# Keeping attention's results transposed, and dividing by the softmax sums on GpSimd

## The chip, the cores and the metric

One program runs on one core of a Trainium2 chip. The metric is the device time of one execution in microseconds (us); the kernel before takes 2816.75 us (median of 3 runs). The core has TensorE (PE; its weight loads are shown as PEld), VectorE (DVE), ScalarE (ACT), GpSimd (POOL) and SyncE (SP, which here only issues DMAs); 16 DMA engines serve them all.

## The reference

A gated cross-attention layer and a two-layer mixture of experts, in float32, on x of shape (8, 512, 256) and a context of shape (8, 1601, 128). What matters here is the attention; it has 16 heads of 16 columns:

```
q, k, v   = heads(x @ Wq + bq), heads(x @ Wk + bk), heads(x @ Wv + bv)
y         = softmax(causal(q k^T / 4)) v                    # SELF
qc, kc, vc = heads(x @ Wcq + bcq), heads(ctx @ Wck + bck), heads(ctx @ Wcv + bcv)
y         = y + softmax(qc kc^T / 4) vc                     # CROSS
x         = x + tanh(g_xattn) * (y @ Wp + bp)
x         = x + tanh(g_ffn) * experts(layernorm(x))         # router, 6 experts top 2, 2 shared, twice
```

Each softmax is computed as exponentials, a product with v, and a division of the result by the sum of the exponentials.

## The kernel before

It has four stages with a barrier between them: `stage_project` (projections to DRAM), `stage_attend`, `stage_mix` (the product with Wp, the layernorm, the first router, and the preparation of expert weights) and `stage_experts`.

`stage_attend` works on 32 items; an item is one batch and a group of 4 heads. The keys of an item are 17 tiles: 13 of context (CROSS, s = 0 to 12) and 4 of x itself (SELF, s = 13 to 16). One list `events`, written by `item_events`, sets the order of TensorE, and VectorE and ScalarE walk the same list. For each tile s, in two halves:

- ST (L847) computes scores transposed, keys on rows; ScalarE's `exp` (L804) takes the exponential into one of three buffers P.
- AV (L862) multiplies with V on TensorE into the PSUM bank OP. V has 16 columns of values and 16 columns of ones for each head, so OP has, on rows 32h to 32h+15, the results of head h transposed, and on rows 32h+16 to 32h+31 its sum, 16 times the same row. OP is [128, 512]: rows by query tokens.
- MAX (L835 and L823, L828) computes scores of the *next* item once more, tokens on rows, into one of the two PSUM buffers R, only for VectorE to take their maxima (L755, L752). 32 such tiles are for CROSS, spread over s = 0 to 12, and 8 for SELF. SHIFT transposes the maxima (L892), which VectorE writes as two rows (L769, L771) that SyncE's DMAs put under the queries (L664).
- OUT, twice an item, for CROSS at (s, half) = (14, 0) and for SELF at (1, 0) of the next item: ScalarE has copied OP to SBUF (`O`, L812); TensorE transposes it back in four pieces (L896) into a buffer R, which it shares with MAX and SHIFT in the order of the list; VectorE takes the reciprocals of the sums, now a column of each head (L776, `den`), and multiplies (L781, `yk`). GpSimd adds the two kinds (L743, `ysum`), and SyncE stores the item (L669) in `y_rows`, tokens on rows.

GpSimd otherwise copies the values into V (L724) and sets the future part of SELF's diagonal tiles to zero (L738), which AV waits for. SyncE's queue has the loads of the item after the next, the shift rows and the stores in one order. At the end a barrier waits for all stores.

In `stage_mix` a block is one batch. Event A loads y (L1125, tokens on rows), transposes it on TensorE in 8 pieces into the PSUM tile `tp` (L1357); ScalarE writes the high part yH (L1310), VectorE the rest yL (L1220). F and FB combine expert weights (L1366, L1377), O multiplies y by Wp (L95 to L97) and VectorE adds and normalises, T transposes the normalised x in two halves through one PSUM tile `xt` (L1403; high part L1323, rest L1258), and G computes the router's logits (L946). The second half of T waits until VectorE has read the first from `xt`.

Of the kernel before, what the change touches and what calls it, by code (L numbers as in the profile page):

```python
# [13 lines left out]
ACT = mybir.ActivationFunctionType  # L14
# [3 lines left out]
P = 128  # L18
# [3 lines left out]
KC = C // P  # L22
# [503 lines left out]
def stage_attend(nc, a, QS, KS, VS, YS, XS, XR, idf, idm, mqm, first):  # L526
# [6 lines left out]
    with ExitStack() as ctx:  # L533
# [9 lines left out]
        O = [r_.sb(f"O{k}", [P, T]) for k in range(2)]  # L543
        den = r_.sb("den", [P, 2, QT, G])
        yk = [r_.sb(f"y{k}", [P, QT, G, D]) for k in range(2)]
        ysum = [r_.sb(f"ysum{u}", [P, QT, GC]) for u in range(2)]
# [9 lines left out]
        (s_v, s_st, s_ex, s_msk, s_av, s_fill, s_drain, s_oe, s_ya, s_pm, s_sr, s_rc) = (  # L556
            r_.sem(n) for n in ("v", "st", "ex", "msk", "av", "fill", "drain", "oe", "ya", "pm", "sr", "rc"))
# [31 lines left out]
        def item_events(n):  # L589
# [3 lines left out]
            for s in range(NKT):  # L593
                for half in range(2):
# [30 lines left out]
        events += [("AV", NI - 1, LAST, halves(LAST)[-1]), ("OUT", NI - 1, SELF)]  # L625
# [4 lines left out]
        slot = {e: k for k, e in enumerate(x for x in events if x[0] in ("MAX", "SHIFT", "OUT"))}  # L630

        with nc.Block() as block:

            @block.sync
            def _(sp):
# [31 lines left out]
                def store(n):  # L667
                    sp.wait_ge(s_ya, n + 1)
                    sp.dma_start(YS[n // NG, :, :, n % NG * GC:(n % NG + 1) * GC], ysum[n % 2][:, :, :]).then_inc(s_yst[n % 2], 16)  # L669
# [14 lines left out]
                for n in range(NI):  # L684
# [20 lines left out]
            def _(pool):  # L705
# [24 lines left out]
                ones(2)  # L730
                for n in range(NI):
                    if n + 1 < NI:
                        values(n + 1)
                    for s in range(CTXT, NKT):
# [5 lines left out]
                    pool.wait_ge(s_drain, slot["OUT", n, SELF] + 1)  # L740
                    if n >= 2:
                        pool.wait_ge(s_yst[n % 2], 16 * (n // 2))
                    pool.tensor_tensor(ysum[n % 2][:, :, :].rearrange("p t c -> p (t c)"),  # L743
                                       yk[0][:, :, :, :].rearrange("p t h d -> p (t h d)"),
                                       yk[1][:, :, :, :].rearrange("p t h d -> p (t h d)"), ALU.add).then_inc(s_ya, 1)

            @block.vector
            def _(dve):
# [25 lines left out]
                def output(n, kind, buf):  # L774
                    t = buf[:, 0, :].rearrange("p (q h e) -> p q h e", q=QT, h=G)
                    dve.reciprocal(den[:, kind], t[:, :, :, D]).then_inc(s_rc, 1)  # L776
                    dve.wait_ge(s_rc, 2 * n + (2 if kind == SELF else 1))
                    if n >= 1:
                        dve.wait_ge(s_ya, n)
                    dk = bcast(den[:, kind].rearrange("p q (h o) -> p (q h) o", o=1), D, 2)  # L780
                    dve.tensor_tensor(yk[kind][:, :, :, :].rearrange("p q h d -> p (q h) d"),  # L781
                                      t[:, :, :, 0:D].rearrange("p q h d -> p (q h) d"), dk, ALU.mult
                                      ).then_inc(s_drain, 1)

                for e in events:
                    if e not in slot:
                        continue
                    k, n = slot[e], e[1]
                    dve.wait_ge(s_fill, k + 1)
                    if e[0] == "MAX":  # L790
                        reduce_tile(n, e[2], k, R[k % 2])
                    elif e[0] == "SHIFT":
                        shift_parts(n, e[2], k, R[k % 2])
                    else:
                        output(n, e[2], R[k % 2])

            @block.scalar
            def _(act):
# [8 lines left out]
                for e in events:  # L807
                    if e[0] == "ST":
                        exp(e[1], e[2], e[3])
                    elif e[0] == "AV" and e[2] in (CTXT - 1, LAST) and e[3] == halves(e[2])[-1]:  # L810
                        act.wait_ge(s_av, av_done[e[1:3]])
                        act.activation(O[kind_of(e[2])][:, :], OP[:, :], ACT.Copy).then_inc(s_oe, 1)  # L812

            @block.tensor
            def _(pe):
# [52 lines left out]
                for e in events:  # L868
# [4 lines left out]
                    if e[0] == "AV":  # L873
                        values(n, e[2], e[3])
                        continue
                    k = slot[e]
# [10 lines left out]
                    elif e[0] == "SHIFT":  # L887
# [5 lines left out]
                    else:  # L893
# [162 lines left out]
def stage_mix(nc, a, YS, X1S, XS, XR, w, BR, SEL, R, tg, idf):  # L1056
# [5 lines left out]
    with ExitStack() as ctx:  # L1062
# [3 lines left out]
        y = [r_.sb(f"y{u}", [P, QT, C]) for u in range(2)]  # L1066
# [11 lines left out]
        tp = r_.ps("tp", [P, KC, T])  # L1078
        op = r_.ps("op", [P, QT, C])
        comb, bias, xt = r_.ps("comb", [P, KC, IW]), r_.ps("bias", [P, KC]), r_.ps("xt", [P, T])  # L1080
# [4 lines left out]
        s_xb, s_T, s_yH, s_yL, s_op, s_x1, s_st, s_ag, s_var, s_rs, s_nm, s_xf = (  # L1085
# [950 lines left out]
```

## Time and profile before

| | us |
|---|---|
| runs (3) | 2814.58, 2816.75, 2819.35; median 2816.75 |
| the profiled execution | 2810.69 |
| its span, first to last instruction | 2808.6 |
| PE busy, in the span | 2489.5 (89%) |
| DVE busy | 1931.8 (69%) |
| ACT busy | 1576.7 (56%) |
| POOL busy | 478.8 (17%) |

The span is what the trace covers; the time of an execution has about 2 us around it. Busy time is a mean over stages with different limits, so the rows below take the stages and then one item of attention by themselves. A line such as L896 is a line of the kernel before.

### The profile page before, as it was taken

To read this page: it belongs to the slowest core of one execution; us is meant where nothing else is said; L and a number is where in the kernel's file an instruction comes from. 1 tells how busy PE (TensorE), PEld (TensorE's weight loads), DVE (VectorE), ACT (ScalarE), POOL (GpSimd) and SP (SyncE) were. 2 spreads that over 40 slices of the span, in tenths; PEclk is the share of its full clock that TensorE was granted. 3 is DMA by queue.
4 is the path that set the end of the run, shared out by engine and by line. 5 is a ranking of instruction groups with operands and counts; after the bars stand their busy time and mean duration, and the time that the engine had idled before them with its cause. 6 is when DMAs were issued, how large, how long until landed. Compare 5 with 4: busy or idle time off the path is not lost. (4 is left out here: it accounts for less than half of the span.)

```text
span 2808.6 us, 55075 instructions
## 1 busy us (share of the span) xinstructions
PE 2489.5 (89%) x20166; PEld 1507.6 (54%) x20166; DVE 1931.8 (69%) x3187; ACT 1576.7 (56%) x3345; POOL 478.8 (17%) x541
## 2 busy tenths in 40 slices
PE   7886999999999999999999998767599968969896
PEld 6773444444444444444444444666487857857675
DVE  8776888888888888888888882544234534634546
ACT  4440777777777777777777776322144423423432
POOL 2002000101010100000010102222303141340413
PEclk9996999999999999999999998768799989989998
DMA  7999757565665647475655623311234312321433
GB/s 267 400 359 237 96 81 104 77 90 75 91 83 85 88 71 104 70 105 67 92 82 85 81 40 90 129 63 57 75 92 120 92 68 61 110 90 35 147 98 98
DMA packets 164962, 305.70 MB, mean 109 GB/s; under 512 B 45607, under 2 KB 112334, under 8 KB 156366
## 3 DMA queue, kind: packets, MB, share of 16 engines
q1 hardware_dynamic: 151358, 265.56, 45.4%
q0 software_dynamic: 12288, 33.57, 3.8%
q10 hardware_dynamic: 1072, 3.23, 0.5%
q8 instruction: 163, 2.67, 0.4%
q14 instruction: 81, 0.66, 0.1%
HBM read 165.13 MB, written 127.68 MB: 104 GB/s over the span
## 5 line engine op out<-in xcount | busy, mean ns | idle before, releaser
L804 ACT ACTIVATE at_P<-at_ST 128x512 f32<-128x512 f32 (+4 forms) x2176 | 1095.9, 559 | 371.8 <-PE at_ST L847 349.5
L755 DVE TENSOR_REDUCE f_part<-at_R 128x2 f32<-128x804 f32 x1024 | 976.0, 994 | 121.1 <-PE at_R L835 117.1
L862 PE MATMUL at_OP<-at_P,at_V 128*32 128x256 f32 x8192 | 641.4, 385 | 16.0 <-ACT at_O L812 12.9
L847 PE MATMUL at_ST<-at_Q,at_K 64*128 64x512 f32 (+4 forms) x1428 | 343.9, 455 | 3.5 <-ACT at_P L804 3.5
L862 PEld LDWEIGHTS at_OP<-at_P,at_V 128*32 128x32 f32 x8192 | 163.1, 108 | 264.0 <-ACT at_P L804 186.7
L835 PE MATMUL at_R<-at_K,at_Q 64*128 64x402 f32 x1344 | 271.0, 392 | 5.1 <-DVE f_part L755 5.1
L738 POOL TENSOR_SCALAR_AFFINE_SELECT at_P<-at_P 128x512 f32<-128x512 f32 x128 | 81.6, 637 | 1088.8 <-ACT at_P L804 1088.8
L847 PEld LDWEIGHTS at_ST<-at_Q,at_K 64*128 64x128 f32 (+1 forms) x1428 | 141.7, 180 | 218.5 <-ACT at_P L804 203.6
L752 DVE TENSOR_REDUCE f_mx<-at_R 128x2 f32<-128x256 f32 (+3 forms) x256 | 209.9, 821 | 42.7 <-PE at_R L828 40.7
L1757 DVE TENSOR_TENSOR ex_ab<-ex_bank,ex_sg 128x256 f32<-128x256 f32 x148 | 62.8, 424 | 239.8 <-ACT ex_sg L1840 182.1
L1700 POOL DMA_INDIRECT ex_gb<-expert_rows,c_IDX x128 | 126.0, 984 | 430.3 <-DMA expert_rows<-ex_rb 314.1
L835 PEld LDWEIGHTS at_R<-at_K,at_Q 64*128 64x128 f32 x1344 | 127.9, 185 | 115.7 <-issue 69.0
L847 PE MATMUL at_ST<-f_Q,f_K 64*128 64x512 f32 (+4 forms) x748 | 180.1, 458 | 2.2 <-ACT at_P L804 2.2
L1840 ACT ACTIVATE ex_sg<-ex_bank 128x256 f32<-128x256 f32 x148 | 57.1, 385 | 207.3 <-PE ex_bank L97 194.4
L835 PE MATMUL at_R<-f_K,f_Q 64*128 64x402 f32 x704 | 150.7, 418 | 15.0 <-DVE f_part L755 9.6
L966 POOL DMA_INDIRECT sorted<-c_XR,c_IDX x128 | 124.8, 975 | 157.4 <-DVE c_IDX L1040 119.1
L95 PE MATMUL ex_bank<-c_WH,ex_xbL 128*128 x296 | 146.7, 496 | 0.0
L95 PE MATMUL ex_bank<-ex_xH,c_WL 128*128 128x512 f32 x256 | 112.0, 437 | 32.3 <-DVE ex_xL L1714 13.4
L847 PEld LDWEIGHTS at_ST<-f_Q,f_K 64*128 64x128 f32 (+1 forms) x748 | 73.7, 182 | 113.8 <-ACT at_P L804 108.9
L96 PE MATMUL ex_bank<-c_WL,ex_xbH 128*128 x296 | 119.9, 405 | 0.0
L97 PE MATMUL ex_bank<-c_WH,ex_xbH 128*128 x296 | 119.7, 404 | 0.0
L835 PEld LDWEIGHTS at_R<-f_K,f_Q 64*128 64x128 f32 x704 | 70.2, 194 | 80.0 <-DVE f_part L755 41.4
(240 smaller groups left out, 4242.6 us busy)
## 6 DMA issues: line engine op xcount, KB each, us to landing
at_K<-k_parts SPq DMA_DIRECT2D x126, 264.1 KB, 9.1
k_parts<-pj_kpart SPq DMA_DIRECT2D x32, 800.5 KB, 9.5
ex_xb<-sorted SPq DMA_DIRECT2D x148, 128.0 KB
expert_rows<-ex_rb SPq DMA_DIRECT2D x148, 128.0 KB
v_items<-pj_vbuf SPq DMA_DIRECT2D x32, 544.0 KB, 9.5
q_parts<-pj_qpart SPq DMA_DIRECT2D x32, 512.0 KB, 11.0
at_Q<-q_parts SPq DMA_DIRECT2D x252, 64.0 KB, 9.8
f_K<-k_parts SPq DMA_DIRECT2D x60, 264.1 KB, 9.5
```

The costliest lines, as they stand in the source:

```text
L95: pe.matmul(out, wL, xH, start=start, stop=False)
L96: pe.matmul(out, wH, xL, start=False, stop=False)
L97: return pe.matmul(out, wH, xH, start=False, stop=stop)
L738: pool.affine_select(out=diag, in_=diag, compare_op=ALU.is_ge, fill=0.0, base=0, pattern=[[0, G], [1, P]], channel_multiplier=-1).then_inc ...
L752: dve.tensor_reduce(mx[:, SELF, :, p, q], buf[:, :, 0:(q + 1) * P], AX.X, ALU.max).then_inc(s_drain, 1)
L755: dve.tensor_reduce(part[:, :, p, q, c], buf[:, :, 0:XC], AX.X, ALU.max).then_inc(s_drain, 1)
L804: act.activation(Pt[(NKT * n + s) % NP][0:rows, h, c0:T], ST[(NST * n + s * G + h) % NB][0:rows, c0:T], ACT.Exp, scale=SCALE).then_inc(s_e ...
L835: ins = pe.matmul(buf[:, h, 0:XC], Q[u][r0:r0 + 64, CROSS, p, q * P:(q + 1) * P], K[u][r0:r0 + 64, p, at:at + XC], start=True, stop=True)
L847: pe.matmul(ST[t % NB][0:rows, c0:T], K[n % NU][half, p, keys], Q[n % NU][half, kind, p, c0:T], start=True, stop=True).then_inc(s_st, 1)
L862: ins = pe.matmul(OP[32 * h:32 * h + 2 * D, at], V[n % 2][0:rows, key_tile(s), h, :], Pt[(NKT * n + s) % NP][0:rows, h, at], start=s in (0 ...
L966: pool.indirect_dma_start(XS[h], bass.IndirectOffsetOnAxis(ap=self.IDX[h][:, j, t:t + 1], axis=0), XR[:, h * self.HT + t, :], None).then_i ...
L1700: pool.indirect_dma_start(gb[n % NGB][j][:, :], None, RS[h], bass.IndirectOffsetOnAxis(ap=R.IDX[h][:, j, t:t + 1], axis=0)).then_inc(s_ga[ ...
```

## The change

In attention, OUT is gone: no transposes, and no reciprocals or products of VectorE on R. Results stay transposed. For all items but the last, GpSimd's queue issues all that follows, in the next item: four DMAs (`sums`) take the row of sums of each head, 2 x 512 numbers, out of `O` and lay it over 32 partitions (`DC`, 128x32). VectorE inverts that tile (event RCP at (5, 0), after the 14th maximum). GpSimd writes it to DRAM (`RC`), loads it back with each head's row repeated on its 32 partitions (`RD`, 128x1024), multiplies `O` by it (128x1024), adds the two kinds (128x512), and SyncE stores the item as [128, 512] in `y_columns` (YT). ScalarE waits with the copy of CROSS's result for the product of the item before (`s_ym`), since `O` is one buffer. The store stands one place later in SyncE's queue. For the last item SyncE issues four SBUF-to-SBUF DMAs for each kind, and VectorE does the reciprocal (on 128x512), products and sum.

In the mix stage y is loaded by four DMAs a batch, already transposed; the eight transposes and `tp` are gone, ScalarE's and VectorE's halves are one instruction each on 128x1024, both from SBUF, and `xt` is two PSUM tiles, so the second half of T no longer waits for the first.

```diff
-                    if (s, half) == (1, 0) and n:
-                        ev.append(("OUT", n - 1, SELF))
-                    if (s, half) == (CTXT + 1, 0):
-                        ev.append(("OUT", n, CROSS))
+                    if (s, half) == (5, 0) and n:
+                        ev.append(("RCP", n - 1))
...
+                if n + 1 < NI:
+                    shift_rows(n + 1, CROSS)
                 if n >= 1:
                     store(n - 1)
-                if n + 1 < NI:
-                    shift_rows(n + 1, CROSS)
-                store(NI - 1)
+                sp.wait_ge(s_ym, NI - 1)
+                for kind in (CROSS, SELF):
+                    sp.wait_ge(s_oe, 2 * NI - kind)
+                    for h in range(G):
+                        sp.dma_start(RD[32 * h:32 * h + D, kind, :], O[32 * h + D:32 * h + 2 * D, kind, :]).then_inc(s_last, 16)
...
+                def sums(n):
+                    pool.wait_ge(s_oe, 2 * (n + 1))
+                    if n >= 1:
+                        pool.wait_ge(s_ri, n)
+                    for h in range(G):
+                        pool.dma_start(DC[32 * h:32 * h + 32, :], O[32 * h + D:32 * h + D + 1, :, :]).then_inc(s_dc, 16)
+                def output(n):
+                    pool.wait_ge(s_ri, n + 1)
+                    pool.dma_start(RC[n], RI[:, :]).then_inc(s_rm, 16)
+                    pool.wait_ge(s_rm, 32 * n + 16)
+                    pool.dma_start(RD[:, :, :], RC[n].rearrange("(h o j) c -> h o (j c)", h=G, o=1).to_broadcast([G, 32, 2 * T])
+                                   ).then_inc(s_rm, 16)
+                    pool.wait_ge(s_rm, 32 * n + 32)
+                    pool.tensor_tensor(yk[:, :, :], O[:, :, :], RD[:, :, :], ALU.mult).then_inc(s_ym, 1)
+                    pool.wait_ge(s_ym, n + 1)
+                    if n >= 2:
+                        pool.wait_ge(s_yst[n % 2], 16 * (n // 2))
+                    pool.tensor_tensor(yT[n % 2][:, :], yk[:, 0, :], yk[:, 1, :], ALU.add).then_inc(s_ya, 1)
                 for n in range(NI):
+                    if n >= 1:
+                        sums(n - 1)
                     if n + 1 < NI:
                         values(n + 1)
+                    if n >= 1:
+                        output(n - 1)
...
-                def output(n, kind, buf):
...
+                def invert(n):
+                    dve.wait_ge(s_dc, 16 * G * (n + 1))
+                    if n >= 1:
+                        dve.wait_ge(s_rm, 32 * n - 16)
+                    dve.reciprocal(RI[:, :], DC[:, :]).then_inc(s_ri, 1)
...
+                        if e[1] >= 1:
+                            act.wait_ge(s_ym, e[1])
+                        act.activation(O[:, kind_of(e[2]), :], OP[:, :], ACT.Copy).then_inc(s_oe, 1)
...
-                        pe.wait_ge(s_oe, 2 * n + (1 if e[2] == CROSS else 2))
-                        for q in range(QT):
-                            ins = pe.transpose(buf[:, 0, q * P:(q + 1) * P], O[e[2]][:, q * P:(q + 1) * P], idf[:, :])
...
-                    sp.dma_start(y[b % 2][:, :, :], YS[b]).then_inc(s_y[b % 2], 16)
+                    for g in range(NG):
+                        sp.dma_start(y[b % 2][64 * (g % 2):64 * (g % 2) + 64, g // 2, :],
+                                     YT[b * NG + g].rearrange("(h e) t -> h e t", h=G)[:, 0:D, :]).then_inc(s_y[b % 2], 16)
...
-                            for t in range(QT):
-                                ins = pe.transpose(tp[:, c, t * P:(t + 1) * P], y[b % 2][:, t, c * P:(c + 1) * P], idf[:, :])
...
-                        if n:
-                            pe.wait_ge(s_xL, n)
+                        if n >= KC:
+                            pe.wait_ge(s_xL, n - KC + 1)
```

## Rows read from the trace of the kernel before

**Rows 1.** Stages: start and end, length, busy us (instructions) per engine, clock, DMA share, GB/s

```profile
290.00:1690.00 1400.00, 1363.46 (x13749) 580.68 (x13745) 1211.63 (x1511) 1080.62 (x2156) 131.40 (x183) 1.00 0.59 83
1735.00:2010.00 275.00, 181.95 (x920) 157.23 (x920) 120.86 (x294) 70.09 (x127) 96.96 (x105) 0.72 0.29 98
```

**Rows 2.** Timeline, ScalarE's copies of OP: start us, us, instruction, idle before

```profile
1010.99 0.63 ACT L812 ACTIVATE at_O<-at_OP 128x512 f32<-128x512 f32 x1
...
1047.23 0.60 ACT L812 ACTIVATE at_O<-at_OP 128x512 f32<-128x512 f32 x1
...
1056.44 0.63 ACT L812 ACTIVATE at_O<-at_OP 128x512 f32<-128x512 f32 x1
```

**Rows 3.** Timeline, TensorE's weight loads of ST around both OUTs of an item

```profile
1012.33 0.19 PEld L847 LDWEIGHTS at_ST<-at_Q,at_K 64*128 64x128 f32 x2 [0.41 <-ACT at_P L804]
...
1017.20 0.19 PEld L847 LDWEIGHTS at_ST<-at_Q,at_K 64*128 64x128 f32 x2 [0.41 <-ACT at_P L804]
...
1048.54 0.19 PEld L847 LDWEIGHTS at_ST<-at_Q,at_K 64*128 64x128 f32 x2 [0.41 <-ACT at_P L804]
...
1050.20 0.19 PEld L847 LDWEIGHTS at_ST<-at_Q,at_K 64*128 64x128 f32 x2 [0.16 <-issue]
...
1051.33 0.19 PEld L847 LDWEIGHTS at_ST<-at_Q,at_K 64*128 64x128 f32 x2 [0.41 <-ACT at_P L804]
```

**Rows 4.** Timeline, VectorE in the same item

```profile
1014.92 0.25 DVE L776 RECIPROCAL at_den<-at_R 128x16 f32<-128x16 f32 x1
...
1015.21 0.42 DVE L781 TENSOR_TENSOR at_y<-at_R,at_den 128x256 f32<-128x256 f32 x1
...
1022.77 3.75 DVE L755 TENSOR_REDUCE f_part<-at_R 128x2 f32<-128x804 f32 x4 [0.18 <-PE at_R L835]
1026.68 1.95 DVE L755 TENSOR_REDUCE f_part<-at_R 128x2 f32<-128x804 f32 x2 [0.16 <-PE at_R L835]
```

**Rows 5.** Timeline, GpSimd: the first mask of the item

```profile
1045.89 0.64 POOL L738 TENSOR_SCALAR_AFFINE_SELECT at_P<-at_P 128x512 f32<-128x512 f32 x1 [28.42 <-ACT at_P L804]
```

**Rows 6.** Busy and DMA share of the item's first 22 us

```profile
1011.00:1033.00 22.00, 21.07 (x199) 8.45 (x195) 20.17 (x25) 16.81 (x32) 1.77 (x2) 1.00 1.04 132
```

**Rows 7.** DMA issues with us to landing: attention's store (1011:1056), ScalarE's load (205:240)

```profile
y_rows<-at_ysum SPq DMA_DIRECT2D x1, 128.0 KB, 12.8
...
f_K<-k_parts ACTq DMA_DIRECT2D x3, 264.1 KB, 6.8
```

**Rows 8.** GpSimd's scatters (ns min/median/max) and their DMA queue in 1876:1900

```profile
L966 POOL DMA_INDIRECT sorted<-c_XR,c_IDX x128: 957/963/1283, 1875.7 to 2521.1; - x128
...
q0 software_dynamic: 768, 2.10, 24.8%
```

**Rows 9.** Timeline, the end of attention

```profile
1729.07 0.60 ACT L812 ACTIVATE at_O<-at_OP 128x512 f32<-128x512 f32 x1 [1.33 <-PE at_OP L862]
...
1732.03 0.56 SPq L669 DMA_DIRECT2D y_rows<-at_ysum  x1
...
1734.79 0.35 SPq L1125 DMA_DIRECT2D mx_y<-y_rows  x1
```

**Rows 10.** SBUF-to-SBUF issues of SyncE (ns), and the landing of attention's stores

```profile
L664 SPq DMA_DIRECT2D at_Q<-at_sh x168: 623/632/1503, 318.1 to 1702.5; - x168
...
DMA to landing us min/median/max: 2.3/12.7/14.8
```

**Rows 11.** Timeline, one block of the mix stage

```profile
1812.10 1.57 PEld L1357 LDWEIGHTS mx_tp<-c_idf,mx_y 128*128 128x128 f32 x8
...
1822.38 0.17 DVE L1250 TENSOR_SCALAR mx_var<-mx_st 128x4 f32<-128x4 f32 x1
...
1825.04 0.69 DVE L1258 TENSOR_TENSOR mx_xL<-mx_xt,mx_xH 128x512 fp32r<-128x512 f32 x1 [1.23 <-ACT mx_xH L1323]
```

**Rows 12.** GpSimd's sums of 128x1024, and VectorE's subtraction from two SBUF tiles (ns)

```profile
L1171 POOL TENSOR_TENSOR c_XR<-c_XR,mx_bp x8: 2342/2347/2805, 1740.7 to 1823.6; 128x1024 f32<-128x1024 f32 x8
...
L1228 DVE TENSOR_TENSOR c_dL<-mx_wd,c_dH x7: 677/685/2873, 1746.3 to 1834.4; 128x512 fp32r<-128x512 f32 x7
```

More of the change, by code:

```diff
@@ L542, in stage_attend @@
         sh = [r_.sb(f"sh{k}", [G * QT, 2, P], F32R) for k in range(2)]
[L543 to L546, printed above, removed]
+        O = r_.sb("O", [P, 2, T])
+        DC, RD = r_.sb("DC", [P, 32]), r_.sb("RD", [P, 2, T])
+        RI = r_.sb("RI", [P, 32])
+        yk, yT = r_.sb("yk", [P, 2, T]), [r_.sb(f"yT{u}", [P, T]) for u in range(2)]
         ST = [r_.ps(f"ST{i}", [P, T]) for i in range(NB)]
@@ L624, in stage_attend @@
             events += item_events(n)
-        events += [("AV", NI - 1, LAST, halves(LAST)[-1]), ("OUT", NI - 1, SELF)]
+        events += [("AV", NI - 1, LAST, halves(LAST)[-1]), ("RCP", NI - 1)]
         av_done = {}
@@ L629, in stage_attend @@
                 av_done["all"] = av_done[e[1:3]] = av_done.get("all", 0) + 1
-        slot = {e: k for k, e in enumerate(x for x in events if x[0] in ("MAX", "SHIFT", "OUT"))}
+        slot = {e: k for k, e in enumerate(x for x in events if x[0] in ("MAX", "SHIFT"))}
         with nc.Block() as block:
@@ L772, in shift_parts, with last_output @@
                                              ).then_inc(s_drain, 1)
-                def output(n, kind, buf):
-                    t = buf[:, 0, :].rearrange("p (q h e) -> p q h e", q=QT, h=G)
-                    dve.reciprocal(den[:, kind], t[:, :, :, D]).then_inc(s_rc, 1)
-                    dve.wait_ge(s_rc, 2 * n + (2 if kind == SELF else 1))
+                def invert(n):
+                    dve.wait_ge(s_dc, 16 * G * (n + 1))
                     if n >= 1:
[L779 to L783, printed above, removed]
-                for e in events:
+                        dve.wait_ge(s_rm, 32 * n - 16)
+                    dve.reciprocal(RI[:, :], DC[:, :]).then_inc(s_ri, 1)
+                def last_output():
+                    for i, kind in enumerate((CROSS, SELF)):
+                        dve.wait_ge(s_last, 16 * G * (i + 1))
+                        dve.reciprocal(RD[:, kind, :], RD[:, kind, :]).then_inc(s_ri, 1)
+                        dve.wait_ge(s_ri, NI + 2 * i)
+                        dve.tensor_tensor(yk[:, kind, :], O[:, kind, :], RD[:, kind, :], ALU.mult).then_inc(s_ri, 1)
+                    dve.wait_ge(s_ri, NI + 3)
+                    dve.wait_ge(s_ya, NI - 1)
+                    dve.wait_ge(s_yst[(NI - 1) % 2], 16 * ((NI - 1) // 2))
+                    dve.tensor_tensor(yT[(NI - 1) % 2][:, :], yk[:, 0, :], yk[:, 1, :], ALU.add).then_inc(s_ri, 1)
+                for e in events:
+                    if e[0] == "RCP":
+                        if e[1] < NI - 1:
+                            invert(e[1])
+                        else:
+                            last_output()
                     if e not in slot:
@@ L886, in _ @@
                         ins = max_tile(n, e[2], buf)
-                    elif e[0] == "SHIFT":
+                    else:
                         if e[2] == CROSS:
@@ L1065, in stage_mix @@
         bp = r_.sb("bp", [P, C])
-        y = [r_.sb(f"y{u}", [P, QT, C]) for u in range(2)]
+        y = [r_.sb(f"y{u}", [P, KC, T]) for u in range(2)]
         x1 = [r_.sb(f"x1{u}", [P, QT, C]) for u in range(2)]
```

77 lines of the change are left out of this document (32 added, 45 removed).

## The prediction

> **What bounds the kernel now.** I read the stages first. In attention TensorE is busy for 1363 of 1400 us at the full clock, VectorE for 1212 (87%), ScalarE for 1081 (77%), GpSimd for 131 (9%) [rows 1]. So half of the program is bound by TensorE, with VectorE close behind and GpSimd nearly free. In time the work is periodic: ScalarE copies SELF's result at 1010.99 and again at 1056.44, an item of 45.45 us, of which 31 follow one another; CROSS's copy is 36.24 us after SELF's [rows 2]. In s = 0 to 12 TensorE and VectorE hold each other: four maxima take VectorE 3.75 us and the next begins 3.91 us after the first [rows 4]. That is the beat, and work taken from both engines should shorten it. In the mix stage nobody is full (TensorE 182 of 275 us, mean clock 0.72) [rows 1]: there chains of waits decide.
>
> **What OUT costs now.** SELF's: from the weight load at 1012.33 to the one at 1017.20 are 4.87 us, with four MAX tiles and OUT; four tiles without it take 3.91 [rows 3, 4]. OUT costs 0.96 there. CROSS's: the half step with it is 1.66 us (1048.54 to 1050.20), the next one, with the same kinds of work, 1.13 [rows 3]: 0.53. Together 1.49 us an item.
>
> **What the change puts in.** On VectorE one reciprocal of 128x32. The one on 128x16 takes 0.25, an operation on 128x4 0.17 [rows 4, 11]: 7 ns for each further element, so 0.17 + 28 x 0.007 = 0.37 us. It stands where VectorE idles only 0.16 us in 3.91 [rows 4]; between 0.2 and 0.4 of it count, I take 0.30. ScalarE's copies and TensorE's other work stay. The net is 1.19 us an item. Items 1 to 30 have all of it (35.7). Item 0 has CROSS's OUT alone (0.5), and the last item both without a beat of maxima (I take 1.1 for 1.49, since no maxima hold TensorE up there). **Attention's loop: -37.3 us.**
>
> **Why I cost the rest of it at nothing.** All else goes beside the loop on GpSimd and the DMA engines, if it is in time. Counted from SELF's copy: the copy ends at 0.6. GpSimd issues four DMAs; nearest are its scatters, 0.96 us each [rows 8]; the last starts at 3.6. Landing is the unknown. In the first 22 us of an item the DMA engines are full (share 1.04) [rows 6]. A store behind SyncE's loads landed after 12.8 us; ScalarE's loads, on a queue of their own beside a busy one, after 6.8; the quickest store after 2.3 [rows 7, 10]. GpSimd also has a queue of its own, so I take 6.8 and keep 2.3 and 12.8 as ends. The sums are there at 10.4 (5.9 to 16.4). VectorE reaches the reciprocal after the 14th maximum, two before 1026.68 being the 15th's start: 15.7 after the copy, 14.7 once SELF's OUT is gone [rows 2, 4]. Behind it wait all the maxima, and TensorE for R. Taken value: no wait. The inverse is there at 15.1; the write of RC lands at 21.9 (17.4 to 27.9); the spread load starts, takes 1.0 to issue, 2.3 to begin and end, and 128 packets of 4 KB. Such a packet takes 24.8% of 16 x 24 us over 512 packets, 0.19 us [rows 8]; eight for each engine are 1.5. It lands at 26.7. The product of 128x1024 takes GpSimd 2.35 [rows 12]: 29.1, the sum of half that size 1.2: 30.3. Two wait for these. ScalarE's CROSS copy comes at 36.2 - 0.7 = 35.5 [rows 2] (0.96 gained by then, 0.30 given back), and behind it stand the exponentials. The first mask is wanted at 34.9 - 0.7 = 34.2 [rows 2, 5]; it is queued behind the sum on GpSimd, and AV waits for it. The cover is thus 6.4 us for the product and 3.9 for the sum; without it, each us late is a us on the item. The V copy, the cheaper store and its later place in SyncE's queue meet no one: the next write to that buffer is two items later, and the shift rows, which SyncE now issues before it, come sooner if anything.
>
> **The end of attention** has no cover. Now the copy ends at 1729.67 and the next stage's first DMA goes at 1734.79: 5.1 us [rows 9]. After: four issues of 0.63 [rows 10], the last starting at 2.0; landed at 4.3 (the 2.3 of an idle queue); the reciprocal of 128x512 at 0.17 + 508 x 0.007 = 3.7 (0.7 if the slope is not real, as other operations of that size take, [rows 12]); product and sum 0.69 each; waits 0.2; store 2.3 and 0.5 to the next stage [rows 9, 10]. That is 12.4. **+7.3 us** (+4 to +9).
>
> **The mix stage.** The eight transposes take 1.57 us a block between G and F [rows 11], and for T's second half VectorE idles 1.23 before L1258 because the first half had to be read first [rows 11]. Both lie on the chain that goes round the block. But O starts nearer to the stretch in which TensorE is at half clock; if the clock rises as late as now, 1.2 us of O run at the lower level, which gives 0.6 back. Per block 1.57 - 0.6 + 1.23 = 2.2. Four blocks in the middle have it (8.8, of which I count one at 1.2 for its missing logits: 7.8); the later ones are led by the router's small steps on VectorE, where I take 2.0 together. At its head, three more loads stand before Wp's in SyncE's queue, between 0.35 and 0.63 each [rows 9, 10], 0.5 taken: +1.5. **-8.3 us** (-15 to +2).
>
> At that head the rows show VectorE's subtraction of two SBUF tiles at 2.87 us instead of 0.69, while GpSimd sums for 2.35 or more [rows 12]. The Trainium skill (SBUF — State Buffer, "Who interferes with whom") says why: a VectorE instruction with two SBUF inputs and a GpSimd instruction that reads SBUF exclude each other for their whole length. yL, which read PSUM so far, now has two SBUF inputs, so by that rule it can be held at the head too, by up to 2.4 us. By the order of the timeline another subtraction was held there already; with the rule counted in full the stage would come to -5.9, without it -8.3.
>
> **Sum.** -37.3 + 7.3 - 8.3 = -38.3. The profiled execution took 2810.7, so it would be 2772.4; the median of the runs is 6 us above it, 2816.75 - 38.3 = 2778.5, and that is the forecast. Its own range is 2764 to 2797: 0.7 to 1.45 us an item, and the ends of the two other terms.
>
> **Rivals.**
>
> *The chain on GpSimd comes late.* For it: the write and the load of RC depend on landings that no row shows for this queue, and the spread load's source has only four different rows outermost. If its packets go by four engines, 32 of them take 6.0 us, not 1.5, and the cover of the sum is gone: it ends at 34.8, 0.6 late. If the write of RC also needs 12.8 us instead of 6.8, the sum is 6.6 late. Against it: at 22 us the loads have ended, and only the write meets them. From 1.2 us of lateness an item (37.3 + 8.3 - 7.3 over 31) the change is slower than before. I price it in the middle, 2.5 us late: 2778.5 + 31 x 2.5 = 2856. Late sums at the reciprocal (16.4 against 14.7, 1.7 an item) would alone take 53 us. The Trainium skill (DMA: Bandwidth & Descriptors, "Rules for kernel authors") speaks against this change: a source whose outermost dimension has fewer than 16 places, a repeating one above all, confines the DMA to that many engines. By that rule the four-engine case is the true one, though with the 6.8 it costs only 0.6 us an item, 2797 in all.
>
> *VectorE keeps the beat.* If TensorE's freed time is idle and only VectorE's own counts, an item gains 0.25 + 0.42 - 0.37 = 0.30 [rows 4], 9.3 in all, and the mix stage half: 2816.75 - 9.3 - 4 + 7.3 = 2811. For it: 3.75 busy of 3.91. Against it: CROSS's OUT lies in SELF's tiles, where VectorE is not full.
>
> *The transposes were hidden, only the tail is seen:* 2816.75 + 7.3 = 2824. Against it stand the 4.87 and the 1.66.
>
> **Chances.** Forecast 0.64, late chain 0.20, VectorE's beat 0.13, hidden 0.03. What a measurement can tell from no change is 0.2%, 5.6 us. Faster takes the forecast and most of the second rival: 0.74; same, 0.05, is the rest of it and a chain that is 1 us late; slower 0.21. The range reaches from the forecast's lower end to VectorE's case, 2764 to 2813, and leaves the late chain's middle out.
>
> **What would show it.** The distance between SELF's copies is 44.3 instead of 45.45; with a late chain it is above 45, and either ScalarE waits for GpSimd's product before its copy, or TensorE's AV for a mask, or VectorE for a DMA before its reciprocal. GpSimd's product ends 27 to 34 us after SELF's copy. From the last copy to the next stage 12 us instead of 5. A block of the mix stage near 15 us instead of 17. A spread load of more than 6 us from first to last packet shows four engines. The forecast is wrong if the distance of the copies moves by less than 0.7 us.

## The result, and the profile after

The changed kernel takes 2855.94 us (median of 4 runs, 2849.15 to 2859.6) against 2816.79 (2814.58 to 2819.35): a ratio of 1.0139, with an interval of 1.0122 to 1.0155. It is slower by 39 us where the forecast had it faster by 38. The profiled execution took 2849.15 us, its span is 2847.3, 38.7 more than before.

Where the 38.7 us lie is read from three times of each trace: the start of the last copy of attention's results, the first DMA of the mix stage, the end.

| us | before | after | difference |
|---|---|---|---|
| start to the last copy | 1729.07 | 1760.93 | +31.9 |
| last copy to the mix stage's first DMA | 5.7 | 12.8 | +7.1 |
| from there to the end | 1073.8 | 1073.6 | -0.2 |

First the stages, by windows (busy time of each engine, then TensorE's granted clock, DMA share and GB/s). The 1400 us of [rows 1] had TensorE busy for 1363 us at the full clock; VectorE, 1212 then, now has less to do and so has TensorE, but the clock is not full any more. The four windows below it are an item with a long wait before the reciprocal (2.45 us), two with middling ones (1.84 and 2.06), and one in which no loads are in flight. The last is the mix stage.

```profile
290.00:1690.00 1400.00, 1317.09 (x13169) 548.49 (x13167) 1150.19 (x1383) 1055.30 (x2105) 312.08 (x386) 0.98 0.63 97
...
750.00:795.00 45.00, 42.12 (x416) 17.39 (x420) 36.13 (x45) 31.44 (x64) 10.32 (x13) 0.92 0.56 86
985.00:1031.00 46.00, 43.17 (x448) 18.03 (x440) 38.38 (x47) 35.25 (x72) 10.53 (x13) 1.00 0.65 97
1031.00:1076.00 45.00, 42.12 (x424) 17.43 (x424) 37.37 (x46) 32.67 (x66) 10.46 (x13) 0.96 0.60 91
1683.00:1726.00 43.00, 42.28 (x434) 17.74 (x434) 36.93 (x45) 34.14 (x69) 10.59 (x13) 1.00 0.12 27
...
1774.00:1925.00 151.00, 97.15 (x515) 89.40 (x515) 87.68 (x199) 48.13 (x85) 43.08 (x48) 0.68 0.39 121
```

SELF's copies are 46.55 us apart on average over 30 items; before they were 45.45 in the item of [rows 2] and 45.48 on average. But items in which VectorE never waits for the sums (three of the 30) take 43.93 to 43.95. So the beat did get shorter, by more than forecast, and waits took 2.6 us an item from it. The waits of attention show which (engine and line, what it waited for: us, times, longest):

```profile
POOL inverse_sums L751 <- DVE at_RI L807: 387.6, 30, 14.5
...
POOL at_yk L756 <- DMA at_RD<-inverse_sums: 222.0, 30, 8.8
...
POOL at_RD L753 <- DMA inverse_sums<-at_RI: 196.5, 29, 8.7
...
PEld at_R L875 <- DVE f_part L784: 126.1, 216, 3.9
...
DVE at_RI L807 <- DMA at_DC<-at_O: 51.1, 26, 3.6
```

GpSimd's waits are long but GpSimd is not what bounds the loop; the line to see is the last. In 26 items VectorE, which the loop cannot do without, stands still before its new reciprocal until the gathered sums have landed, and TensorE then stands before the next maxima. One item's timeline (start, us, engine, line, operation, idle before it). Its SELF copy starts at 985.39:

```profile
986.28 2.02 POOL L746 DMA_DIRECT2D at_DC<-at_O  x4 [3.56 <-ACT at_O L852]
...
1002.44 0.56 POOL L751 DMA_DIRECT2D inverse_sums<-at_RI  x1 [13.04 <-DVE at_RI L807]
1009.87 0.71 POOL L753 DMA_DIRECT2D at_RD<-inverse_sums  x1 [6.86 <-DMA inverse_sums<-at_RI]
1017.64 2.38 POOL L756 TENSOR_TENSOR at_yk<-at_O,at_RD 128x1024 f32<-128x1024 f32 x1 [7.06 <-DMA at_RD<-inverse_sums]
1020.09 1.27 POOL L760 TENSOR_TENSOR at_yT<-at_yk 128x512 f32<-128x512 f32 x1
1021.32 0.63 POOL L773 TENSOR_SCALAR_AFFINE_SELECT at_P<-at_P 128x512 f32<-128x512 f32 x1
```

```profile
1001.79 0.35 DVE L807 RECIPROCAL at_RI<-at_DC 128x32 f32<-128x32 f32 x1 [1.84 <-DMA at_DC<-at_O]
```

The four gathers are issued by 2.9 us after the copy's start and land at 12.5 to 16.4; VectorE reaches the reciprocal at 14.6 and goes on at 16.4. The product ends at 34.6, the sum at 36.0, and the first mask follows at once. The prediction wanted it at 34.2; but the wait at the reciprocal has moved the whole item by 1.84, to 36.0, so here the late sum costs nothing beside it. How long each DMA of this chain takes (issue durations in ns, then us to landing over all items, min/median/max; first the gathers, the write of the inverses, the spread load):

```profile
L746 POOL DMA_DIRECT2D at_DC<-at_O x124: 496/501/778, 330.6 to 1728.7; - x124
...
DMA to landing us min/median/max: 1.6/12.5/15.4
```

```profile
L751 POOL DMA_DIRECT2D inverse_sums<-at_RI x31: 562/562/567, 348.4 to 1733.4; - x31
...
DMA to landing us min/median/max: 1.7/7.1/8.9
```

```profile
L753 POOL DMA_DIRECT2D at_RD<-inverse_sums x31: 706/706/729, 355.0 to 1735.4; - x31
...
DMA to landing us min/median/max: 7.6/7.9/9.5
```

The minima of the first two come from items 29 and 30, where SyncE has no loads in flight (DMA share 0.12 in 1683:1726 above). A gather of 4 KB lands there within 1.6 to 2.3 us; behind the loads it takes 12.5. The spread load is different: its longest time, 9.5, is in one of those quiet items, so its length is its own. Its 10 us there, by queue:

```profile
DMA packets 529, 0.54 MB, mean 54 GB/s; under 512 B 400, under 2 KB 400, under 8 KB 528
...
q0 software_dynamic: 528, 0.53, 16.9%
```

16.9% of 16 x 10 us are 27 us of packets. Spread over 16 engines they would be over in 1.7 us; they took about 7, so about four engines carried them.

The wait of 1.7 us (51.1 over 30) is not all that an item lost: the windows of 750:795 and 1031:1076 have a granted clock of 0.92 and 0.96 between the two levels, so part of them ran at 1.2 GHz, and what TensorE did before was stand still for the maxima. The item from 749.2 waited 2.45 us and took 4.8 more than an undisturbed one. The item of the timeline above kept the full clock (1.00 in 985:1031): it took 45.85, which is 1.9 more than an undisturbed one for its wait of 1.84. So it is in nearly all items whose clock stayed at 1.00: they lose their wait and nothing else, also where the mask follows late. In 17 of the 30 items the clock fell, and the loss above the wait lies in these (one item apart, the one from 1355, in which TensorE stood 1.2 us for nothing that the profile shows).

The end of attention and the mix stage's head, which answer to [rows 9]:

```profile
1760.21 3.35 DVE L812 RECIPROCAL at_RD<-at_RD 128x512 f32<-128x512 f32 x1 [27.08 <-DMA at_RD<-at_O]
...
1765.41 3.35 DVE L812 RECIPROCAL at_RD<-at_RD 128x512 f32<-128x512 f32 x1 [1.12 <-DMA at_RD<-at_O]
```

```profile
1770.29 0.34 SPq L707 DMA_DIRECT2D y_columns<-at_yT  x1
1773.74 2.37 SPq L1163 DMA_DIRECT2D mx_y<-y_columns  x4
...
1780.15 3.87 SPq L1163 DMA_DIRECT2D mx_y<-y_columns  x4
```

In the mix stage the blocks are 15.1 us apart in the middle (17.1 before, by the starts of their first products of y with Wp), as forecast. Yet the scatters, which begin when the blocks are done, start 140.7 us after the stage's first DMA and started 141.0 after it before. From the first block's first product to the eighth's it takes 105.5 us instead of 116.1, but the first of them comes 25.9 us after the stage's first DMA instead of 15.9: what the blocks gained was lost at the head. There the y load is now four DMAs whose outermost dimension has 4 places with rows of 2 KB, and the first 27 us of the stage moved 160 GB/s instead of 237:

```profile
DMA packets 4781, 4.31 MB, mean 160 GB/s; under 512 B 1263, under 2 KB 4134, under 8 KB 4780
...
mx_wd<-in_Wd SPq DMA_DIRECT2D x3, 256.0 KB, 9.4
```

and before:

```profile
DMA packets 5607, 6.39 MB, mean 237 GB/s; under 512 B 1351, under 2 KB 4965, under 8 KB 5605
...
mx_wd<-in_Wd SPq DMA_DIRECT2D x4, 256.0 KB, 5.2
```

The second expert weight lands at 22.6 us after the stage's first DMA instead of 13.1, and TensorE waits for it:

```profile
1796.41 3.78 PE L1394 MATMUL mx_comb<-mx_wg,mx_upT 128*128 128x256 f32 x8 [4.91 <-DMA mx_wd<-in_Wd]
```

### The profile page after: what moved, and what is told of

The parts are those of the page before. It is cut to its first block and busy times, and to the rows that moved or that the text cites. A ratio compares the mean times of both kernels' runs of the same rounds, so it can differ in the third digit from the quotient of the medians.

```text
span 2847.3 us, 54566 instructions
## 1 busy us (share of the span) xinstructions
PE 2462.1 (86%) x19846; PEld 1478.4 (52%) x19846; DVE 1910.1 (67%) x3087; ACT 1574.8 (55%) x3337; POOL 671.6 (24%) x757
## 5 line engine op out<-in xcount | busy, mean ns | idle before, releaser
L902 PE MATMUL at_OP<-at_P,at_V 128*32 128x256 f32 x8192 | 655.0, 392 | 15.9 <-ACT at_O L852 12.9
L756 POOL TENSOR_TENSOR at_yk<-at_O,at_RD 128x1024 f32<-128x1024 f32 x31 | 73.6, 2373 | 229.7 <-DMA at_RD<-inverse_sums 229.7
```

What stands on the lines that cost most here:

```text
L756: pool.tensor_tensor(yk[:, :, :], O[:, :, :], RD[:, :, :], ALU.mult).then_inc(s_ym, 1)
L902: ins = pe.matmul(OP[32 * h:32 * h + 2 * D, at], V[n % 2][0:rows, key_tile(s), h, :], Pt[(NKT * n + s) % NP][0:rows, h, at], start=s in (0 ...
```

## The experiments

Two theories of the attention loop. A: the gathers are late at VectorE's reciprocal, and this wait alone is what the loop loses. B: the spread load, on four engines, brings the product and sum too late for CROSS's copy and the first mask. C is about the mix stage: the y loads' form holds back the weights. All these kernels ran on chips where before takes 2680 us. Against the runs above, the part from the mix stage's first DMA to the end is 131 us shorter there (942.9 us in e3_rcp7_rd4, 1073.6 in the changed kernel) and attention is the same (undisturbed items take 43.9 us on both), so each is compared with before on its own chip.

**Reciprocal later (e1_rcp7).**

```
-                    if (s, half) == (5, 0) and n:
+                    if (s, half) == (7, 0) and n:
```

> The changed kernel with one edit: VectorE's reciprocal of the sums stands at (7, 0) instead of (5, 0), 5.8 us later in the item. Theory A (the four small gathers land late, VectorE stands at the reciprocal for about 2 us, TensorE behind it, and each stall also costs a stretch at half clock; nothing else is late): VectorE's wait for the gathers is gone, all items come to 43.95 to 44.1 us instead of 46.55, no half-clock stretch is left in attention, time about 2856 - 31 x 2.5 = 2778. Theory B (the rest of the chain on GpSimd has no slack either): reciprocal at 20.3 after SELF's copy, write of the inverses landed at 26, spread load at 34, product ends at 36.7, sum at 38; CROSS's copy (wanted at 35.3) and the first mask (wanted by 35.5) are 1.4 and 2.5 us late, so items stay at 46 to 46.5 and the time at 2840 to 2856. I hold B likelier.

Measured: 2702.11 us against 2680.69, ratio 1.0085 (1.0065 to 1.0105). VectorE reaches the reciprocal 20.5 us after the copy and waits for nothing; the write of the inverses, now behind most of the loads, lands after 3.7 us instead of 7.1. But the inverse is there 4 us later than in the changed kernel, the spread load lands at 31 to 36, the sum ends at 37.4 at the median, and the wait has moved to ScalarE's copy and the values. In this kernel's waits:

```profile
POOL at_yk L756 <- DMA at_RD<-inverse_sums: 234.4, 31, 9.2
...
PE at_OP L902 <- ACT at_O L852: 40.9, 48, 3.6
ACT at_O L852 <- POOL at_yk L756: 28.7, 19, 3.6
```

Items are 45.97 us. A alone is not the whole: without its wait, B's decides.

**Spread load as four DMAs (e2_rd4).** Each copies 32 rows' worth to 32 partitions with an outermost dimension of 32.

```
-                    pool.dma_start(RD[:, :, :], RC[n].rearrange("(h o j) c -> h o (j c)", h=G, o=1)
-                                   .to_broadcast([G, 32, 2 * T])).then_inc(s_rm, 16)
+                    for h in range(G):
+                        row = RC[n, 32 * h:32 * h + 32, :].rearrange("(o j) c -> o (j c)", o=1)
+                        pool.dma_start(RD[32 * h:32 * h + 32, :, :].rearrange("p k t -> p (k t)"),
+                                       row.to_broadcast([32, 2 * T])).then_inc(s_rm, 16)
```

> The changed kernel with one edit: the spread load is four DMAs, one for each head, whose source repeats one row 32 times, so that the outermost dimension is 32 and not 4. If four DMA engines carry the spread load now, it lands 4.5 to 5.5 us after its start instead of 7.9; if the number of engines was not the limit, it stays at 7 to 8. Theory A (the wait at the reciprocal decides): the items stay at 46.5 us, the time at 2850 to 2857. Theory B (the late product and sum decide): items get 1 to 2 us shorter, time 2800 to 2825.

Measured: 2724.86, ratio 1.0167 (1.0144 to 1.019). The same bytes are there 4.5 us after the first of four issues instead of 7.9 (medians), although the issues take 1.25 us longer; the product ends at 31.7 us, the sum at 33.1, in time for both. It changes nothing for the better: items are 46.82 us, since the wait at the reciprocal (54.8 us over 25 items, up to 5.9) stands where it stood. This also shows that in the changed kernel the late product and sum cost nothing yet: taken away, they give nothing back. B alone is not the whole either.

**Both (e3_rcp7_rd4).**

> The changed kernel with both edits: reciprocal at (7, 0), spread load as four DMAs. Both theories: no wait at the reciprocal, product ended at about 33 and sum at 34.3 after SELF's copy, before CROSS's copy and the mask want them; items of 43.95 to 44.2 us, full clock throughout attention, time 2775 to 2785. If the items stay above 45, something else in the loop costs (traffic, GpSimd's port), and both theories are wrong.

Measured: 2640.28, ratio 0.985 (0.9834 to 0.9867), 40 us faster than before. One item of it, SELF's copy at 987.8, and its 1400 us of attention:

```profile
1008.97 0.56 POOL L751 DMA_DIRECT2D inverse_sums<-at_RI  x1 [17.11 <-DVE at_RI L809]
1013.55 1.96 POOL L755 DMA_DIRECT2D at_RD<-inverse_sums  x4 [4.03 <-DMA inverse_sums<-at_RI]
1018.09 2.39 POOL L758 TENSOR_TENSOR at_yk<-at_O,at_RD 128x1024 f32<-128x1024 f32 x1 [2.58 <-DMA at_RD<-inverse_sums]
1020.56 1.27 POOL L762 TENSOR_TENSOR at_yT<-at_yk 128x512 f32<-128x512 f32 x1
```

```profile
290.00:1690.00 1400.00, 1358.16 (x13841) 567.46 (x13833) 1185.30 (x1425) 1114.91 (x2226) 368.24 (x499) 1.00 0.64 99
```

The sum ends 34.0 us after the copy, the clock is full, items are 44.00 us on average (43.9 in all but four), and the last copy is at 1682.5 instead of 1760.9. Either mend alone leaves the kernel slower than before; together they give 40 us, the size of the forecast's gain, though not by its parts: the last copy comes 46.6 us earlier than in the trace of before instead of 37.3, and the mix stage gives nothing instead of 8.3. The two waits stand one behind the other, and the later one decides.

**The loads held back (e6_loads).** With the four-DMA spread load and the reciprocal where the change has it, SyncE issues the next loads only when the gathers have landed.

```
                     if n + 2 < NI:
+                        if n >= 1:
+                            sp.wait_ge(s_dc, 16 * G * n)
                         load(n + 2)
```

> The changed kernel with the spread load as four DMAs, the reciprocal at (5, 0) as in the change, and SyncE's loads of the item after the next held until the gathers of the sums have landed (a wait on their semaphore before the loads). If contention with those loads makes the gathers late, they land 4 to 5 us after SELF's copy as in the last two items, VectorE does not wait, and items come to 44 us, unless the inverses' write and the spread load, now in the middle of the loads, come late: product at 33.6, sum at 35, just in time. Time 2777 to 2800. If the gathers are late for another reason (GpSimd's descriptors, the queue itself), they still land at 14 to 17 and the time stays near 2855.

Measured: 2804.62, ratio 1.0482 (1.045 to 1.0515), the slowest of all. The gathers did land in time, which shows that the loads are what delays them (this kernel, gathers):

```profile
L748 POOL DMA_DIRECT2D at_DC<-at_O x124: 496/502/774, 329.2 to 1804.0; - x124
...
DMA to landing us min/median/max: 1.5/1.6/3.2
```

VectorE no longer waits before the reciprocal. But the loads now fly when the inverses are written, and that small DMA takes what the gathers took:

```profile
986.12 0.56 POOL L753 DMA_DIRECT2D inverse_sums<-at_RI  x1 [11.10 <-DVE at_RI L811]
999.74 1.96 POOL L757 DMA_DIRECT2D at_RD<-inverse_sums  x4 [13.06 <-DMA inverse_sums<-at_RI]
```

13.6 us at the median, the sum ends at 37 to 42 and items are 49.1 us. The contention was moved, not removed. A second cost came with this edit, and neither expectation names it: SELF's shift rows stand behind the loads in SyncE's queue, and in 28 items TensorE waits for them before SELF's scores, up to 5.1 us (65.9 us in all; the changed kernel has no such wait). This kernel's waits:

```profile
PEld at_ST L891 <- DMA at_Q<-at_sh: 39.4, 18, 5.1
...
PEld at_ST L891 <- DMA f_Q<-at_sh: 21.5, 9, 4.9
```

So the run shows what delays the gathers, but its 4.8% are the price of both, and how much is the late sum's alone is not shown.

**The y loads compact (f1_compact), on top of both mends.** y_columns keeps only the 64 rows that carry y; a batch's y is then one DMA over 128 rows of 4 KB.

```
-    YT = nc.dram_tensor("y_columns", [NI, P, T], F32).ap()
+    YT = nc.dram_tensor("y_columns", [NI, GC, T], F32).ap()
...
-                    sp.dma_start(YT[n], yT[n % 2][:, :]).then_inc(s_yst[n % 2], 16)
+                    for h in range(G):
+                        sp.dma_start(YT[n, D * h:D * h + D, :], yT[n % 2][32 * h:32 * h + D, :]).then_inc(s_yst[n % 2], 16)
...
-                    for g in range(NG):
-                        sp.dma_start(y[b % 2][64 * (g % 2):64 * (g % 2) + 64, g // 2, :],
-                                     YT[b * NG + g].rearrange("(h e) t -> h e t", h=G)[:, 0:D, :]).then_inc(s_y[b % 2], 16)
+                    sp.dma_start(y[b % 2][:, :, :], YT[b * NG:(b + 1) * NG].rearrange("(k g) c t -> (g c) k t", k=KC)
+                                 ).then_inc(s_y[b % 2], 16)
```

> Changed against the kernel with the later reciprocal and the four spread DMAs: y_columns holds only the 64 rows that carry y, and one item's store is four DMAs of 16 rows, so a batch's y load is one DMA over 128 rows of 4 KB instead of four whose outermost dimension is 4. Theory C (the four y loads run on few DMA engines and hold back the weight loads that stand behind them in SyncE's queue, which costs the mix stage's head what its blocks gain): y's load lands some 4 us after its issue, the second expert weight load lands some 8 us earlier, and the time from the mix stage's first DMA to the end falls by about 8 us, so the time is 0.982 of before instead of 0.985. Rival D (the head waits for something else, and the blocks' gain ends at the experts' steps whatever the loads do): y lands earlier, the time from the first DMA to the end stays within 2 us. The attention loop keeps its 43.9 us an item either way; if the four stores of 16 rows disturb it, items get longer.

Measured: 2629.3 against 2679.75, ratio 0.9809 (0.9789 to 0.9828). From the mix stage's first DMA to the end it takes 928.5 us; the kernel with both mends took 942.9 there. The first 27 us of the stage in this kernel:

```profile
DMA packets 6562, 6.81 MB, mean 252 GB/s; under 512 B 1379, under 2 KB 5408, under 8 KB 6560
...
mx_wd<-in_Wd SPq DMA_DIRECT2D x4, 256.0 KB, 5.3
```

The second weight lands at 13.7 us (23.8), the scatters begin at 130.7 (141.5). The first block's first product comes 16.4 us after the stage's first DMA. C holds, and is worth 14 us by these parts and 10.5 by the medians of this kernel and f2_tail (below), which ran on the same chip with the y loads as they were. In the profiled executions 4.3 of the 14 are lost before the mix stage (last copy at 1686.7 instead of 1682.5); the traces do not show why. The edit changes three things at once: the outermost dimension, the length of the rows and the number of issues (SyncE issues for 2.4 and 3.9 us in the first two rounds of four, for 0.4 us a batch here). What the outermost dimension alone is worth is not shown.

**The same alone on the changed kernel (h2_compact).**

> The changed kernel as it is, with y_columns of 64 rows and one y load per batch only. The attention loop stays as in the changed kernel (46.5 us an item, late gathers, late spread load), so the kernel stays slower than before; theory C alone gives back 9 to 11 us in the mix stage: ratio to before about 1.0135 less 0.004, 1.010. Rival: with the four small stores added to SyncE's queue while gathers are late, items get longer than 46.5 us and the gain is gone.

Measured: 2706.86 against 2682.18, ratio 1.0101 (1.0074 to 1.0127). Items stay at 46.6 us, from the stage's first DMA to the end it takes 930.4. The attention loop and the mix stage's head are two separate losses.

**One PSUM tile for the transposes (f3_xt1), on top of both mends.**

```
-[r_.ps(f"xt{c}", [P, T]) for c in range(KC)]
+[r_.ps("xt", [P, T])] * KC
```

> Changed against the kernel with the later reciprocal and the four spread DMAs: the mix stage's transposes go back to one PSUM tile for both columns of a block, as in the kernel before the change. Theory (the second tile is what lets TensorE go on while ScalarE and GpSimd take the first): blocks of the mix stage go from 15.0 us back to about 16.2, and the time from the mix stage's first DMA to the end grows by 5 to 8 us. Rival (the head's late weights hide what the blocks give, as the unchanged length of the two stages together suggests): blocks get longer, the end moves by under 2 us.

Measured: 2642.62 (2640.71 to 2650.81), ratio 0.9869 (0.9843 to 0.9895), against 0.985 with two. The blocks are 15.9 to 16.6 us apart and the scatters begin 4 us later, but the end comes only 2 us later. So the second tile is worth about 1 us a block, near the forecast's 1.23, and half of that is lost behind it. The 2 us are within what the two ratios leave open.

**The last item's sums moved by TensorE (f2_tail), on top of both mends.** One product per kind with columns 16 to 127 of the identity replaces SyncE's DMAs within SBUF.

```
-                        sp.dma_start(RD[32 * h:32 * h + D, kind, :], O[32 * h + D:32 * h + 2 * D, kind, :]).then_inc(s_last, 16)
+                                pe.matmul(R[i][0:P - D, 0, :], idf[:, D:P], O[:, kind, :], start=True, stop=True).then_inc(s_last, 1)
```

> Changed against the kernel with the later reciprocal and the four spread DMAs: for the last item SyncE's eight DMAs within SBUF that move the sums down by 16 rows are replaced by one TensorE product per kind with 112 columns of the identity, which writes the moved sums to PSUM; VectorE's reciprocals and products take 112 rows from there. Theory: of the 12.2 us from the last copy's end to the next stage's first DMA, the two reciprocals of about 3.35 us and two products stay, and the DMAs' issue and landing (about 4 us) become a product of some 1 us: about 9 us, the kernel 3 to 4 us faster, ratio to before about 0.984. Rival: VectorE's two long reciprocals set the end anyway (they could start before the last copy only for CROSS), and the tail falls by under 1.5 us.

Measured: 2639.76, ratio 0.9845 (0.9824 to 0.9865): no gain. From the last copy's start to the next stage it takes 13.6 us, with the DMAs 12.8. The rival was nearer: two reciprocals set the end. What neither saw is that the edit itself puts both of them behind the last copy. Both products stand behind all of TensorE's other work, so CROSS's reciprocal, which with the DMAs began 0.3 us before the last copy, now begins 1.1 us after its start (its row is the product's, 1687.66 - 3.35):

```profile
1687.66 0.69 DVE L811 TENSOR_TENSOR at_yk<-at_O,at_RD 112x512 f32<-112x512 f32 x1
1688.27 3.35 DVE L809 RECIPROCAL at_RD<-at_R 112x512 f32<-112x512 f32 x1
1691.65 0.69 DVE L811 TENSOR_TENSOR at_yk<-at_O,at_RD 112x512 f32<-112x512 f32 x1
```

The last copy starts at 1683.25; two reciprocals and two products stand in a row behind it.

**All mends (f4_all).**

> All mends in one kernel: the reciprocal at a later place of the item, the spread load as four DMAs of 32 rows, y_columns with 64 rows and one y load per batch, and the last item's sums moved by TensorE. If the parts add: 40 us less than before from attention and the short blocks, 8 from the y loads, 3 to 4 from the end of attention, a ratio of about 0.981 to before. If the head does not wait for the y loads, about 0.984.

Measured: 2629.88, ratio 0.9808 (0.9787 to 0.9828), the same as f1_compact, as the flat result of f2_tail makes it.

**All mends, CROSS's product early (h1_early).** It is issued right after the first values of SELF.

> All mends together, and for the last item CROSS's sums are moved by TensorE right after the first SELF values instead of behind the last ones, so that CROSS's reciprocal and product are done when SELF's copy ends. Theory (in the version before, TensorE's order held the first of the two reciprocals until 1.7 us after the last copy began, so that two of 3.35 us stood in a row): one reciprocal of 3.35 us and two products are left, the next stage's first DMA comes about 9.5 us after the last copy's start instead of 13.6, and the kernel is 4 us faster than with all mends before: ratio to before about 0.979. Rival (the store's landing sets it, not VectorE): under 1.5 us.

Measured: 2631.59 (2627.25 to 2633.41), ratio 0.9818 (0.9794 to 0.9843). The profiled execution has the tail near to what was expected, 10.2 us from the last copy's start (1683.56) to the next stage's first DMA (1693.75) instead of 13.6:

```profile
1683.43 0.69 DVE L813 TENSOR_TENSOR at_yk<-at_O,at_RD 112x512 f32<-112x512 f32 x1
1685.36 3.36 DVE L811 RECIPROCAL at_RD<-at_R 112x512 f32<-112x512 f32 x1 [1.24 <-PE at_R L912]
```

But CROSS's product stands in TensorE's row now and the last copy comes 6.9 us after CROSS's instead of 5.8. Counted from CROSS's copy the gain over the version before is 2.4 us, and the timed runs do not tell it from none. The best version is thus the one with both mends and the compact y, with or without the new tail: 1.9% faster than before, and about 3% faster than the change as it came (an estimate, 0.9809 / 1.0139 = 0.967, since the two ratios are from different chips).

## Why the prediction was wrong

Step by step, as it put them:

- *OUT costs 1.49, the reciprocal 0.30, an item gets 1.19 shorter: 44.3 us.* Right in kind, a little small: undisturbed items are 43.94, a gain of 1.5 net. The reciprocal of 128x32 takes 0.35 (0.37 estimated).
- *The sums are there at 10.4 (5.9 to 16.4). Taken value: no wait.* **This step failed.** The landing was taken as 6.8 us, because GpSimd has a queue of its own [rows 7]. It is 12.5, nearly that of the store behind SyncE's loads (12.8 in the same rows), whose end of the range the prediction had worked out: 16.4 against 14.7, 1.7 an item. That is what the runs show, 16.5 at the median item and 1.7 on average, and the agreement is in part luck: the last of the four gathers, which decides, was issued at 2.4 instead of 3.6 and landed 14.0 us after its issue instead of 12.8. A row with share 1.04 [rows 6] said that all engines were taken, and the row of the slower landing was the one from that very stretch; ScalarE's 6.8 came from another stage. The kernel with the loads held back shows that it is the loads: 1.6 us without them.
- *The issues of the gathers take 0.96 each.* They take 0.50; this helped by 1.2 us.
- *The write of RC 6.8.* It takes 7.1.
- *The spread load takes 1.5 us of packets, landed after 4.8.* **Mis-sized too**: 7.9 us, since about four engines carry it. The prediction had this case as a rival's first half, with 6.0 us for 1.5. The Trainium skill (DMA: Bandwidth & Descriptors, "Rules for kernel authors") gives the rule: a source with fewer than 16 places outermost, a repeating one for example, is confined to at most that many engines. The trace agrees: 27 us of packets in about 7. By it alone the sum is at 34.8; with the later inverse it was at 36.3. In the changed kernel this cost nothing, since the wait at the reciprocal moves the demand as well (e2_rd4); e1_rcp7 shows what a late product and sum cost once that wait is gone.
- *Each us late is a us on the item.* Right in items that kept the full clock, too little in the others. Measured against the undisturbed 43.94, 1.7 us of wait cost 2.6 on average. The rest is nearly all the granted clock, 0.98 over the loop: by an estimate 2% of 46.55 us, 0.9 us an item. It is full again in e3_rcp7_rd4. Late masks have no part in it: without them e2_rd4 loses 2.9 us an item for 1.8 us of wait.
- *The end of attention +7.3, 12.4 in all.* Right: from the last copy's end 12.2, from its start +7.1. The reciprocal of 128x512 takes 3.35 (3.7 estimated).
- *The mix stage -8.3: 2.2 a block, the head +1.5.* **Failed as well**: the blocks were right (15.1 us, 10.6 us gained up to the eighth, where 9.8 were forecast), the head was not, +10.0 instead of +1.5. The step counted three more issues and took the y load's transfer as unchanged. The rule that the prediction weighed for the spread load applies to these loads too, outermost 4, and was not put to them; f1_compact measures the form of the loads as a whole, 10 to 14 us.
- *yL may be held by GpSimd's additions at the head, by up to 2.4.* It was: the first yL takes 3.37 us, the median of the eight is 1.23. With that rule (the Trainium skill, SBUF — State Buffer, "Who interferes with whom") the trace agrees: GpSimd's sum beside it ends at 1789.6, and yL 1.1 us later. It did not decide: it ends at 1790.7, and TensorE's wait for the weights at 1796.4.

The sum with measured terms: +31.9 + 7.1 - 0.2 = +38.8. The first is about -46.5 (31 x 1.5) for the shorter beat and +78 (30 x 2.6) for the waits. The late-chain rival was the true case, at 0.20; its 2.5 us late and its 2856 us came out almost to the number, in part by luck. Its price was for the write of RC and the spread load; what decided were the gathers, which it had beside it at 53 us; and two errors cancel in its sum: it has attention's loop at +40.2 (-37.3 and 31 x 2.5) where +31.9 was measured, and the mix stage at -8.3 where it was -0.2.

## What to carry to other kernels

When a change moves work onto small DMAs beside a loop whose loads fill the DMA engines, take the landing from a row in that stretch, not from a queue that was idle, and place the consumer by it; a queue of its own did not help here (12.5 us against the 12.8 of SyncE's store). For each DMA that is added or changed count the places of its outermost dimension, also for those that feed the next stage. And where a chain has two unknown landings one behind the other, mending either may show nothing: try both before giving up the change. When loads are held back, look at what else stands behind them in their queue.

## What the runs showed of the hardware

- A 4 KB DMA of GpSimd's queue lands after 1.6 us (median in e6_loads, where SyncE's loads wait for it) and after 12.5 (median, up to 15.4) beside SyncE's loads, when the DMA share is 1.04 [rows 6]. Its 16 KB write lands after 1.7 us with no loads, 7.1 in the changed kernel and 13.6 in e6_loads, where the loads start before it.
- The spread load of 512 KB, which about four engines carried, cut in four DMAs with an outermost dimension of 32 each: 7.9 us become 4.5, with 1.25 us more of issue time (4 x 0.49 instead of 0.71).
- VectorE's reciprocal takes 0.25 us for 128x16, 0.35 for 128x32, 3.35 for 128x512: 6.3 ns for each further element of a partition, whereas a product of 128x512 takes 0.69.
- A short stand of TensorE, once in an item of 45 us, can bring stretches at the 1.2 GHz level. In the changed kernel the items with waits of 1.5 us and more before the reciprocal had a granted clock of 0.93 to 0.97 in 17 cases (waits of 1.55 to 3.56) and of 1.00 in six (1.75 to 2.13). Where it stayed at 1.00 an item lost its wait; where it fell, 1.3 to 2.6 us more.
